# Last-layer weight operations in halves, earlier value weights and earlier value evictions in the first two attentions of a four-layer decoder kernel

## The reference

```
x = x + tanh(g_xattn[0]) * _L0_xattn_ref(_layernorm(x), ctx_4096, Wq, Wk, Wv, Wo)
x = x + tanh(g_ffn[0])   * _L0_ffn_ref(_layernorm(x), ...)
...
x = x + tanh(g_ffn[3])   * _L3_ffn_ref(_layernorm(x), w_gate, w_up, w_down)
```

```
scores = jnp.einsum('bkgqd,bksd->bkgqs', q, k) * scale
attn = jax.nn.softmax(scores.astype(jnp.float32), axis=-1)
out = jnp.einsum('bkgqs,bksd->bkgqd', attn, v)
return out @ Wo.T
```

```
amax = jnp.max(jnp.abs(xb), axis=-1, keepdims=True)
scale = jnp.exp2(jnp.floor(jnp.log2(amax)) - EMAX)
q = _quant_elem(xb / scale, mbits) * scale
```

## Time and profile before

| what | value |
|---|---|
| median of the runs (2) | 1351.64 us (1351.39 to 1351.9) |
| the profiled execution | 1352.49 us, span 1350.8 us |
| mean granted TensorE clock | 0.972 |
| PE busy | 1211.8 us, 90% of the span |
| DVE busy | 901.2 us, 67% |
| ACT busy | 638.6 us, 47% |
| POOL busy | 530.1 us, 39% |
| A0, first to last scores | from 26.20 us to 586.36 us |
| A1, first to last scores | from 660.21 us to 964.33 us |

### The profile page before, as it was taken

The page is one execution under the profiler, slowest core; times in us unless marked ns, Lnnn a source line. Parts: engine busy times, 40 slices in busy tenths (PEclk is TensorE's granted clock), DMA queues, the critical chain, the costliest instruction groups (busy, mean ns, idle before and its releaser), DMA issues.

```text
span 1350.8 us, 19317 instructions
## 1 busy us (share of the span) xinstructions
PE 1211.8 (90%) x7154; PEld 949.9 (70%) x7154; DVE 901.2 (67%) x1638; ACT 638.6 (47%) x1046; POOL 530.1 (39%) x385
## 2 busy tenths in 40 slices
PE   6899998788998899989989988889799999999986
PEld 5777787667876787778777877877686444677743
DVE  6578778765488778765647875487465775433287
ACT  3465555444355455641345543356325777432252
POOL 5127364662236565615222545134263300345312
PEclk9999999989899999989989999899899999999999
DMA  5487778664387788870157875286804000192000
GB/s 203 67 160 153 152 151 162 121 148 94 72 146 157 145 162 146 151 166 20 51 105 134 164 142 118 48 146 114 180 1 136 1 1 1 53 234 95 0 1 32
DMA packets 356189, 146.38 MB, mean 108 GB/s; under 512 B 327745, under 2 KB 334049, under 8 KB 356097
## 3 DMA queue, kind: packets, MB, share of 16 engines
q1 hardware_dynamic: 356096, 145.15, 51.1%
HBM read 57.17 MB, written 5.37 MB: 46 GB/s over the span
## 4 chain that ended last, share of the span: by engine, by line
PE 67%; DVE 22%; issue 4%; ACT 3%; POOL 2%; DMA 2%; SPq 0%; DVEq 0%; ACTq 0%; POOLq 0%
PE ps L850 13%; PE ps L878 8%; PE ps L804 6%; DVE p L1119 6%; PE ps L819 6%; PE ps L795 6%; DVE rows_and_turned L1106 5%; PE ps L1957 5%; PE ps L1523 3%; PE ps L1549 3%; PE ps L1970 2%; PE ps L781 2%; PE ps L2255 1%; DVE rows_and_turned L1035 1%; PE ps L1505 1%
## 5 line engine op out<-in xcount | busy, mean ns | idle before, releaser
L850 PE MATMUL ps<-kT,qT 128*128 128x512 f32 (+3 forms) x1152 | 241.0, 345 | 64.6 <-DVE p L1119 62.4
L850 PEld LDWEIGHTS ps<-kT,qT 128*128 128x128 f32 (+1 forms) x1152 | 201.2, 191 | 122.3 <-DVE p L1119 63.8
L1106 DVE TENSOR_REDUCE rows_and_turned<-ps 128x1 f32<-128x768 f32 x192 | 183.4, 955 | 151.2 <-PE ps L850 151.1
L974 ACT ACTIVATE ps<-ps,rows_and_turned 128x768 f32<-128x768 f32 x192 | 168.0, 875 | 210.1 <-DVE rows_and_turned L1106 209.8
L982 ACT ACTIVATE p<-ps,rows_and_turned 128x768 f16<-128x768 f32 x192 | 172.9, 900 | 174.7 <-ACT ps L974 99.2
L878 PE MATMUL ps<-pT,vv 128*128 128x256 f16 (+1 forms) x1728 | 230.1, 281 | 10.5 <-DMA pT<-p 6.6
L1119 DVE SCALAR_TENSOR_TENSOR p<-ps,rows_and_turned,p 128x768 f16<-128x768 f32 x192 | 193.4, 1007 | 7.1 <-ACT p L982 7.1
L878 PEld LDWEIGHTS ps<-pT,vv 128*128 128x128 f16 (+1 forms) x1728 | 173.1, 110 | 32.7 <-issue 14.1
L713 POOL TENSOR_TENSOR wo<-raw,one 128x512 fp32r<-128x512 f32 (+1 forms) x48 | 51.5, 1072 | 288.1 <-PE ps L819 223.9
L804 PE MATMUL ps<-xT,wq 128*128 128x512 f32 x528 | 144.8, 410 | 0.0
L819 PE MATMUL ps<-wo,oT 128*128 128x512 f32 (+1 forms) x396 | 113.9, 412 | 4.4 <-DVE x L1018 3.3
(11 more groups left out here) (276 smaller groups left out, 1940.1 us busy)
## 6 DMA issues: line engine op xcount, KB each, us to landing
raw<-in_l_wq SPq DMA_DIRECT2D x44, 256.0 KB, 3.4
f2raw<-in_f_w SPq DMA_DIRECT2D x11, 776.0 KB, 4.7
rows_and_turned<-in_m_w SPq DMA_DIRECT2D x11, 768.0 KB, 5.3
raw<-in_l_wo SPq DMA_DIRECT2D x32, 256.0 KB, 3.3
pT<-p SPq DMA_TRANSPOSE x192, 3.7
raw<-in_l_wo SPq DMA_DIRECT2D x16, 192.0 KB, 3.3
w3gu<-rows_and_turned SPq DMA_DIRECT2D x11, 256.0 KB, 3.0
ctxraw<-in_ctxT SPq DMA_DIRECT2D x2, 1024.0 KB, 7.6
```

Source lines behind the costliest of these rows:

```text
L850: last = nc.tensor.matmul(sc[:, lo:hi], query(A, h, qp)[:, r * P:(r + 1) * P], keys(A, h // A.g)[0:hd, kp, b, lo:hi], start=(qp, kp) == PA ...
L974: nc.scalar.activation(score_banks(n), score_banks(n), ACT.Exp, bias=nmax[:, n % 32:n % 32 + 1], accum_out=rsum[:, n % 32:n % 32 + 1]).the ...
L1106: nc.vector.tensor_reduce(nmax[:, n % 32:n % 32 + 1], sc[:, 0:S], AX.X, ALU.max, negate=True).then_inc(sem("att_nmax"), 1)
```

## The change

Seven things change, all of them in the two attentions:

- `need`: the second pair of value weights is due 24 steps ahead, not 16.
- `near`, `amax_at`, `scale_at`, `step_at`: the maxima, the scaling and the rounding step of a tile are done in two halves of 768 columns. The maxima of the halves stand at the ends of steps 4h + 2 and 4h + 3 (both at 4h + 4 where the tile before belongs to head h - 2), the scaling at 4h + 6 and 4h + 8, the rounding step at 4h + 9 and 4h + 10. The three operations on 128 x 48 come once, after the second half's maxima; the small one on the block scale (1056) once, in the first half.
- The tile's load is issued one step later, at 4h' + 9.
- The heads of A0's tiles become (2, 6, 10, 14, 18, 22, 24, 26).
- The semaphore counts that SP and POOL wait for follow from the halves.
- On PE, the two small products of the value scale (859, 863) come after the inner pieces and the products of step n - 5, not ahead of them.
- On DVE, the evictions of V pieces that ended the step before come ahead of the maximum; all other evictions stay behind it.

```diff
-        need += [(RT * self.g * u + (-6 if u == 0 else -16), p, ("v", u, p)) for u in range(0, kv, 2) for p in range(2)]
+        need += [(RT * self.g * u + (-6 if u == 0 else -24), p, ("v", u, p)) for u in range(0, kv, 2) for p in range(2)]
...
-            self.amax_at[RT * h + 4], self.scale_at[RT * h + 7], self.step_at[RT * h + 8] = n, n, n
-            self.load_weights_at[RT * (tiles[i - 1] if i else h - 4) + 8], self.store_at[RT * h + 16] = n, n
+            near = i and tiles[i - 1] == h - 2
+            for part in range(2):
+                self.amax_at[RT * h + 2 + part + (2 - part if near else 0), part] = n
+                self.scale_at[RT * h + 6 + 2 * part, part], self.step_at[RT * h + 9 + part, part] = n, n
+            self.load_weights_at[RT * (tiles[i - 1] if i else h - 4) + 9], self.store_at[RT * h + 16] = n, n
...
-A0 = Attention("l0", 32, 4, 128, (2, 6, 10, 12, 18, 20, 22, 26), 0, None)
+A0 = Attention("l0", 32, 4, 128, (2, 6, 10, 14, 18, 22, 24, 26), 0, None)
...
-                    sp.wait_ge(sem("w3_scaled"), n)
+                    sp.wait_ge(sem("w3_scaled"), 2 * n)
...
-                    g.wait_ge(sem("w3_step"), n * 3 + 3)
+                    g.wait_ge(sem("w3_step"), n * 5 + 5)
...
+                for what in inner:
+                    job_in_turn(what)
+                if n >= LAG:
+                    weighted(n - LAG)
                 if n in A.scale_steps:
                     value_scale_turned(A.scale_steps[n])
                 if n - 1 in A.scale_steps:
                     value_scale_spread(A.scale_steps[n - 1])
-                for what in inner:
-                    job_in_turn(what)
-                if n >= LAG:
-                    weighted(n - LAG)
...
-                nc.vector.tensor_reduce(w3amax[:], blocks(w3in[:]), AX.X, ALU.max,
+                nc.vector.tensor_reduce(half(w3amax, part), blocks(half(w3in, part)), AX.X, ALU.max,
                                         apply_absolute_value=True).then_inc(sem("w3_small"), 1)
-                v.wait_ge(sem("w3_small"), n * 4 + 1)
+                if part == 0:
+                    return
+                v.wait_ge(sem("w3_small"), n * 5 + 2)
...
-                nc.vector.scalar_tensor_tensor(blocks(w3y[:]), blocks(w3in[:]), 2.0, per_block(w3inv[:]), ALU.mult,
+                nc.vector.scalar_tensor_tensor(blocks(half(w3y, part)), blocks(half(w3in, part)), 2.0,
+                                               per_block(half(w3inv, part)), ALU.mult,
...
             for n, inner, end in A.steps:
+                for what in ended:
+                    if what[0] == "V":
+                        job(what)
                 if n < A.items:
                     maximum(n)
...
                 for what in ended:
-                    job(what)
+                    if what[0] != "V":
+                        job(what)
```

More of the change, by code:

```diff
@@ L1031, in job, with half, block_maxima @@
                                                    ALU.subtract).then_inc(sem("att_w"), 1)
[L1033 to L1035 removed]
+            def half(ap, part):
+                n = ap.shape[1] // 2
+                return ap[:, part * n:(part + 1) * n]
+            def block_maxima(n, part):
+                if part == 0:
+                    v.wait_ge(sem("w3_raw"), n * 16 + 16)
+                nc.vector.tensor_reduce(half(w3amax, part), blocks(half(w3in, part)), AX.X, ALU.max,
                                         apply_absolute_value=True).then_inc(sem("w3_small"), 1)
[L1037 removed]
+                if part == 0:
+                    return
+                v.wait_ge(sem("w3_small"), n * 5 + 2)
                 nc.vector.tensor_scalar(w3amax[:], w3amax[:], 2.0 ** -100, None, ALU.max).then_inc(sem("w3_small"), 1)
[L1039 removed]
+                v.wait_ge(sem("w3_small"), n * 5 + 3)
                 nc.vector.tensor_scalar(w3inv[:].bitcast(U32), w3amax[:].bitcast(U32), EXP, EXP,
@@ L1153, in att_dve @@
                     value_scale_spread(A.scale_steps[n - 1])
-                if n in A.amax_at:
-                    block_maxima(A.amax_at[n])
-                if n in A.scale_at:
-                    scale_weights(A.scale_at[n])
-                if n in A.step_at:
-                    step_of_weights(A.step_at[n])
+                for part in range(2):
+                    if (n, part) in A.amax_at:
+                        block_maxima(A.amax_at[n, part], part)
+                    if (n, part) in A.scale_at:
+                        scale_weights(A.scale_at[n, part], part)
+                    if (n, part) in A.step_at:
+                        step_of_weights(A.step_at[n, part], part)
             outputs(A.pairs - 1)
```

21 lines of the change are left out of this document (10 added, 11 removed).

## The result

| what | before | after |
|---|---|---|
| median of the runs | 1351.64 us | 1322.38 us (2 runs, 1321.81 to 1322.96) |
| ratio to before, 95% interval | | 0.9768 (0.9739 to 0.9798) |
| profiled execution, span | 1352.49, 1350.8 us | 1322.96, 1321.2 us |
| mean granted TensorE clock | 0.972 | 0.974 |
| A0, first to last scores | 560.16 us | 541.89 us |

A forecast was written before the change was run, and what follows sets the result against it. PE was taken to set the pace in most steps, DVE where last-layer work is slipped in. Seven terms summed to -26.8 us from 1352.49, giving 1325.7, put as 1325; own range 1318 to 1332, overall 1306 to 1339.

The forecast's parts named there:

- likeliest case: Whole kernel: the summed forecast of 1325 us, own range 1318 to 1332, chance 0.45.
- 1, tile 3 off the value weights: A0 steps 52 to 58: without last-layer work there, the waits around POOL's value-weight splits and rounding go, -10.9 us.
- 2, scale steps of A0: A0 steps 60 to 62: no net gain, as tile 3's second maxima delay the query eviction; +0.4 us, bounds -3 and +3.
- 3, tiles in halves: Tiles 0, 1, 2, 4, 5, 8, 10: a tile costs 3.1 us, not 4.6; together -14.0, bounds -28 and -7.
- 4, tiles 6 and 7: A0 steps 92 to 114: POOL's work just fills four steps, DVE waits about 2.4 at step 110; +2.3 us, bounds -3 and +6.
- 5, scale steps of A1: A1 steps 28 to 34: tile 9's second maxima fall behind the reduce of step 27; loss 8.8 for 6.9, +1.9 us.
- 6, value evictions first: A0 steps 4, 68, 70, A1 steps 4, 36, 38: evictions ahead of the maximum close or shorten PE's gaps; -12.8 us.
- 7, the same at step 1: Step 1, both attentions: DVE waits for ACT, PE's gap grows from 1.5 to 3.1 us, lower clock added; +6.3 us.
- first rival: Halves slip between POOL's splits without waits, tiles cost 1.1 us; 19 us less, 1306; chance 0.22.
- The second: Rival: halving gains nothing, gaps at steps 60, 28, 110 cost clock, step 100 adds 2 us; 1339 us, chance 0.18.
- The third: Rival: value evictions find PE bound by something else and tiles cost as before; 1351 us, chance 0.10.
- slower rival: Store and queued transfers hold up PE 5 us or more at each of 11 tiles; 1380 us, chance 0.05.

The follow-up runs named there:

- list14: Kernel before, with only A0's fourth last-layer weight tile moved from head 12 to head 14: 1344.05 us, 0.9919 of the kernel before.
- only_v_first: Kernel before, with only VectorE's evictions of V pieces put ahead of the next maximum: 1339.33 us, 0.9901 of the kernel before.
- v00_late: Changed kernel, with each attention's first value piece again evicted behind maximum, remainder and outputs: 1320.0 us, 0.9763 of the kernel before.
- v16: Changed kernel, with the second group's value weights split at -16 again, not -24: 1330.93 us, 0.9817 of the kernel before.
- near_small: Changed kernel, with the 128x48 operations of heads 24 and 26 moved to steps 103 and 111, first scaling half behind them: 1320.4 us, 0.9754 of the kernel before.
- reduce48: Changed kernel, with every tile's three 128x48 tensor_scalar operations replaced in place by reductions (block scales come out wrong): 1308.11 us, one execution.
- all_small: Changed kernel, with 128x48 operations one step later, and for heads 24 and 26 ahead of first scaling (steps 103, 111): 1302.96 us, 0.9624 of the kernel before.
- spread: Changed kernel, 128x48 operations moved, first value eviction late; also second scaling and rounding halves one step later except two-head followers: 1298.01 us, 0.9586, beside 0.9588 without.

## Why the prediction came out

The forecast was 1325, the result 1322.4, inside its own range and by its likeliest case. That it came so near is in part luck: terms 3 and 6 gained 6.3 and 3.0 us more than was put, terms 2, 4 and 5 lost 1.4, 4.3 and 1.1 more, so misses of 16 us in all leave 2.7; and on another chip the same kernel took 1329.55. The terms, from the starts of scores in the two profiled executions:

| term | predicted | measured | where |
|---|---|---|---|
| 1, tile 3 off the value weights | -10.9 | -10.8 | A0 52 to 59 |
| 2, scale steps of A0 | +0.4 | +1.8 | A0 60 to 62 |
| 3, tiles in halves | -14.0 | -20.3 | 0, 1, 2, 4, 8, 10: -14.1; 5: -6.2 |
| 4, tiles 6 and 7 | +2.3 | +6.6 | A0 92 to 114, less 1.3 of tile 5 |
| 5, scale steps of A1 | +1.9 | +3.0 | A1 28 to 34 |
| 6, value evictions first | -12.8 | -15.8 | A0 4 to 9, 68 to 70, A1 3 to 5, 36, 38 |
| 7, the same at step 1 | +6.3 | +6.0 | steps 1 and 2, both |
| sum | -26.8 | -29.5 | the loops -28.7, the executions -29.5 |

**Terms 1, 6 and 7** held in mechanism, and each was shown by itself: list14, only_v_first and v00_late. Of the two edits behind term 1 only the tile's place in the list counted (v16). In term 6 the gaps were sized right, and the lower clock behind the Q evictions was left out: the two of A1 gained 2.3 and 2.0 us where 0.65 was put for each, those of A0 0.5 and 0.7. Step 70 is what the prediction had said: the eviction at 341.53 lies in DVE's idle time, where it was behind maximum and remainder in the earlier trace rows.

```profile
341.53 0.75 DVE L1033 SCALAR_TENSOR_TENSOR vv<-ps,rows_and_turned,vv 128x512 f16<-128x512 f32 x1 [1.99 <-ACT vv L973]
342.91 2.80 PEld L798 LDWEIGHTS ps<-wv,xT 128*128 128x128 f32 x24
343.03 2.88 PE L798 MATMUL ps<-wv,xT 128*128 128x256 f32 x24
```

**Term 3** was a tile at 3.1 us in place of 4.6. Tile 0 costs 2.5 (33.49 for nine steps of 3.44). The small operation beside a split did take 1.20 us, as read from the earlier trace rows, and steps 12 and 13 cost 1.3 where 1.5 was put; the second scaling half 0.8 in place of 1.1; the rounding halves the 0.5. At tile 2 the small operations all but missed the split in this execution (step 44 took 3.85 us, in v00_late's 4.97), and at tile 10, where a stretch at the lower clock went with the old wait, the gain was 4.8 in place of 3.1. The term was right in kind and a third too small. (Its best case of 1.1 us a tile was added up from 0.4 and 0.6, so it is 1.0.)

**Term 4** is the step that was mis-sized, beyond its bound of +6. The prediction looked for the wait at the scaling of step 110 and put 1.4 us for each tile's maxima; it had the row of a small operation that lasts as long as a split, the rule beside it that the same happens behind a rounding pass of 3.5 us, and used that only for a rival. The term did not ask what POOL does during step 100, where both maxima and then the small operations stand: the rounding of the tile before, two heads back. The kernel before has the very thing, where heads 18 and 20 follow each other, in the tail of a pass:

```profile
418.06 2.76 POOL L691 TENSOR_TENSOR rows_and_turned<-rows_and_turned 128x1536 bf16<-128x1536 bf16 x1
...
419.96 0.91 DVE L1038 TENSOR_SCALAR rows_and_turned<-rows_and_turned 128x48 f32<-128x48 f32 x1
```

Two such waits, 3.46 and 2.75 us, are where the gap of 6.89 us behind step 101 and the lower clock of step 102 came from; near_small and reduce48 removed both, one by another place and one by another form. The 110 wait did not show since the small operations had waited already; with reductions it does (2.85). The sum written for the term doesn't come out either: 1.4, 1.1 and 0.5 for each of two tiles and the wait of 2.4 make 8.4 us, not 10.5, which needs 1.1 for each scaling half. The stretch lost 14.8 without tile 5, and in four other executions with this code it was 0.9 to 1.5 us longer still, at the clock of step 110.

**Terms 2 and 5** had their mechanism (maxima of tile 3 and tile 9 behind the reduce of the value weights, PE's gap 4.26 where 3.2 to 4.4 was given, 4.19 in A1), and what was left out is again the clock of the next steps. With the small operations moved away, the two gaps are 2.67 and 2.38 us.

The first rival (no waits on POOL, 1306) was wrong for the change as made, and is what the kernel becomes when the waits are taken away: 1303 with all_small. The second had the mechanism of step 100 at 2 us, where steps 101 and 102 cost 9.1 more than in near_small. The third (the evictions advance nothing) fell with the gap of step 70. Of the slower rival (the store, PE waiting for transfers) nothing shows: PE's waits for transfers in front of the products of probabilities and values are the same as before, two and 6.6 us in all.

## What to carry to other kernels

Before a small DVE operation is put in a slot that 'costs nothing', look at what POOL runs there: its price is not its own 0.2 us but what is left of POOL's instruction beside it, so long POOL passes and small elementwise DVE operations belong in different steps, or the operation in a form that takes no part in it. Where work moves on one engine, list what the other engine then meets one tile later; spread won 3.1 us at four places and paid 5.8 at four others. And price a gap of PE with the clock after it, as a chance: a gap shorter by 1.57 us gave back 3.06.

## What the runs showed of the hardware

- The wait between DVE and POOL goes by the kind of operation, not its size: tensor_scalar on 128 x 48 took 3.46 us beside a pass of 3.46 us and 0.17 to 0.19 alone, a reduction on the same values 0.20 beside such a pass, scalar_tensor_tensor with both inputs in SBUF 1.91 beside a split and 0.94 alone. Over the thirteen traces with tensor_scalar, all 118 of these 128 x 48 operations that took over 0.3 us ended within 0.05 us of the POOL instruction beside them. While POOL runs pass after pass, one waiting DVE operation gets in between two of them, then the next waits for the pass that has begun (3.46, 0.19 and 2.75 us in step 101).
- PE's lower clock after a gap depends on more than the gap: behind the gap of 2.57 us at step 4 the step took 8.24 us in one execution of the changed kernel and 6.70 in another, behind the 1.55 of step 1 of A0 step 2 took 8.11 in every trace that has it, behind 3.12 it took 9.5 to 9.6 in all but one, and 8.11 there. In A1 step 2 took 7.88 behind a gap of 1.54 in five traces and 9.51 in one, and 9.5 or 11.0 behind 2.86. Such a fall costs 1.5 us, or 3.1 where it lasts twice as long. It is also what sets executions apart: in the two loops the changed kernel had 54.6 us at half clock and v16 71.7, and half of that difference, 8.5 us, is most of the 9.7 by which v16's loops are longer.
